# Decoder layer on one core: in the looped head groups VectorE turns the values in 32x32 blocks, and GpSimd takes their low part

## The reference, cut to what matters

```python
q = (hidden_states @ w_q).reshape(B, S, Hkv, g, D)
k = (hidden_states @ w_k).reshape(B, S, Hkv, D)
v = (hidden_states @ w_v).reshape(B, S, Hkv, D)
scores = jnp.einsum('bqhgd,bkhd->bhgqk', q, k) * scale
scores = jnp.where(causal, scores, -jnp.inf)
probs = jax.nn.softmax(scores.astype(jnp.float32), axis=-1).astype(q.dtype)
attn = jnp.einsum('bhgqk,bkhd->bqhgd', probs, v)
return attn.reshape(B, S, Hq * D) @ w_o
```

## Time and profile before

| | before |
|---|---|
| median of 3 runs | 735.61 us (734.72 to 736.96) |
| profiled execution, its own time | 735.36 us |
| its span, first to last instruction | 733.6 us |
| TensorE busy | 710.6 us, 97% |
| VectorE busy | 565.9 us, 77% |
| ScalarE busy | 379.1 us, 52% |
| GpSimd busy | 381.1 us, 52% |

### The profile page before, as it was taken

One profiled execution on the slowest core, in us unless ns is written; L12 is line 12 of the kernel. 1 busy time (PEld: TensorE's weight loads), 2 busy tenths in 40 slices (PEclk: granted clock), 3 DMA queues, 4 the chain that ended last, 5 costly groups with the idle time before them and its releaser, 6 DMA issues.

```text
span 733.6 us, 11238 instructions
## 1 busy us (share of the span) xinstructions
PE 710.6 (97%) x3494; PEld 590.4 (80%) x3494; DVE 565.9 (77%) x1166; ACT 379.1 (52%) x962; POOL 381.1 (52%) x373
## 2 busy tenths in 40 slices
PE   7999999999999999999999999999999889999994
PEld 6788888888888888888888888888887657888873
DVE  7588868876886787688768877885368878898897
ACT  4365426534643664365436535561656565655642
POOL 4565426443552555165426525542435535789885
PEclk9999999999999999999999999999999999999998
DMA  9513027204600550152035002401910002222003
GB/s 296 169 59 116 1 93 215 66 0 144 214 16 13 149 202 0 67 178 79 0 114 180 20 0 97 154 0 44 327 46 1 1 1 57 87 60 64 29 12 114
DMA packets 44901, 63.91 MB, mean 87 GB/s; under 512 B 4462, under 2 KB 23278, under 8 KB 44878
## 3 DMA queue, kind: packets, MB, share of 16 engines
q1 hardware_dynamic: 44878, 63.62, 27.4%
HBM read 52.67 MB, written 10.95 MB: 87 GB/s over the span
## 4 chain that ended last, share of the span: by engine, by line
PE 86%; DVE 6%; POOL 2%; issue 2%; ACT 2%; DMA 0%; POOLq 0%; DVEq 0%; ACTq 0%
PE psum L490 20%; PE psum L492 20%; PE psum L491 20%; PE psum L622 7%; PE psum L710 5%; PE psum L711 5%; PE psum L733 2%; PE psum L732 2%; DVE stats L1257 1%; PE psum L496 1%; PE psum L510 1%; ACT probs L912 1%; POOL o_sum L1217 1%; DVE xprobs L1383 1%; DVE negmax L1448 0%
## 5 line engine op out<-in xcount | busy, mean ns | idle before, releaser
L1154 POOL TENSOR_TENSOR probs<-probs,rowinv 128x512 f32<-128x512 f32 x64 | 76.4, 1193 | 239.7 <-DVE rowinv L1454 239.7
L1403 DVE STREAM_TRANSPOSE pt<-probs 32x128 f32<-32x128 f32 x560 | 169.0, 302 | 13.9 <-POOL pt_lo L1165 7.0
L912 ACT ACTIVATE probs<-probs,negmax 128x128 f32<-128x128 f32 x256 | 99.8, 391 | 137.9 <-DVE negmax L1448 137.9
L490 PE MATMUL psum<-xt_hi,wq_hi 128*128 128x512 f32 x256 | 103.4, 404 | 0.0
L490 PE MATMUL psum<-wo_hi,at_hi 128*128 128x512 f32 x256 | 100.4, 392 | 0.5 <-DVE at_lo L1459 0.5
L492 PE MATMUL psum<-xt_hi,wq_lo 128*128 128x512 f32 x256 | 99.9, 390 | 0.0
L491 PE MATMUL psum<-xt_lo,wq_hi 128*128 128x512 f32 x256 | 99.8, 390 | 0.0
L492 PE MATMUL psum<-wo_hi,at_lo 128*128 128x512 f32 x256 | 99.7, 390 | 0.0
L491 PE MATMUL psum<-wo_lo,at_hi 128*128 128x512 f32 x256 | 99.6, 389 | 0.0
L1393 DVE TENSOR_TENSOR xacc<-psum,xacc 128x512 f32<-128x512 f32 x64 | 44.1, 689 | 64.5 <-PE psum L492 64.5
L1165 POOL TENSOR_TENSOR pt_lo<-pt,pt_hi 128x512 fp32r<-128x512 f32 x56 | 71.9, 1285 | 27.5 <-ACT pt_hi L968 27.5
(11 more groups left out here) (149 smaller groups left out, 1530.1 us busy)
## 6 DMA issues: line engine op xcount, KB each, us to landing
wq_raw<-in_L_attn_w_q SPq DMA_DIRECT2D x8, 1024.0 KB, 5.5
wo_raw<-in_L_attn_w_o SPq DMA_DIRECT2D x8, 1024.0 KB, 7.8
u_zn<-zeros_gu SPq DMA_DIRECT2D x16, 344.0 KB, 6.4
unpacked_w<-u_q SPq DMA_DIRECT2D x8, 688.0 KB, 7.8
gw<-unpacked_w SPq DMA_DIRECT2D x20, 256.0 KB, 3.5
unpacked_w<-u_q SPq DMA_DIRECT2D x6, 512.0 KB, 6.5
u_q<-in_L_ffn_gate_qweight SPq DMA_DIRECT2D x8, 344.0 KB, 5.8
u_q<-in_L_ffn_up_qweight SPq DMA_DIRECT2D x8, 344.0 KB, 4.0
```

The source lines that it names most:

```text
L490: pe.matmul(dst, a_hi, b_hi, start=start, stop=False)
L912: e = act.activation(probs[:, t % 2, j, :], probs[:, t % 2, j, :], ACT.Exp, bias=negmax[:, t % 2, j:j + 1], accum_out=rowsum[:, t % 2, j:j ...
L1154: pool.tensor_tensor(probs[:, t % 2], probs[:, t % 2], rowinv[:, t % 2, :].unsqueeze(2).to_broadcast([P, HG, P]), ALU.mult).then_inc(prob_ ...
L1403: turned = dve.transpose(pt[keys, :, queries], probs[queries, t % 2, :, keys])
```

## The change

For the seven looped groups the turning moves from TensorE to VectorE. `vt` gets room for both halves, and a new buffer `v_raw` takes the turned block in SBUF. VectorE's new `turn_values` makes 16 transposes per half, each of 32 partitions by 4x32 elements, so that one instruction turns a 32x32 block of each of the four tiles; the table `TURN_V` deals them out over slots 2 to 5 (5, 5, 4 and 2 of them, half 1) and 8 to 10 (4, 6 and 6, half 0), at the end of VectorE's slot. ScalarE writes `v_hi` from `v_raw` at the start of its slots 6 and 11 (`SPLIT_V`), and GpSimd, no longer VectorE, subtracts: `v_lo` from `v_raw` and `v_hi`, at the start of its slots 6 and 11. For slot 11 the loops of ScalarE and GpSimd get one slot more. The first v block, ahead of the loop, and the one in `last_group` are turned by TensorE as before.

```diff
-    TURN_V = {2: 1, 6: 0}
+    TURN_V = {2: (1, 0, 5), 3: (1, 5, 10), 4: (1, 10, 14), 5: (1, 14, 16), 8: (0, 0, 4), 9: (0, 4, 10), 10: (0, 10, 16)}
+    SPLIT_V = {6: 1, 11: 0}
...
-            vt = sb("vt", [P, HALF])
+            vt = sb("vt", [P, 2, HALF])
+            v_raw = sb("v_raw", [P, BH, P])
...
@@ TensorE, group
-                    for k, i in enumerate(FILL.get(t, ())):
+                    for i in FILL.get(t, ()):
                         fill(g, i)
-                        if k == 0 and t in TURN_V:
-                            turn_values(g, TURN_V[t])
...
@@ ScalarE
+            def values_rounded(g, n):
+
+                act.wait_ge(v_turned, g * NH + (2 - n))
+                act.wait_ge(pv_done, g * NB + (0 if n == 1 else BH) + PRIME)
+                act.copy(v_hi[:, n * BH:(n + 1) * BH, :], v_raw[:]).then_inc(vt_hi, 1)
...
                 if unit == "v":
-                    act.wait_ge(vt_done, g * NH + (2 - n))
+                    act.wait_ge(vt_done, 1)
+                    act.wait_ge(v_turned, g * NH)
...
-                for t in range(SLOTS):
+                for t in range(SLOTS + 1):
+                    if t in SPLIT_V:
+                        values_rounded(g, SPLIT_V[t])
                     if t < NB:
                         exponentials(g, t)
-                    for k, i in enumerate(FILL.get(t, ())):
+                    for i in FILL.get(t, ()):
                         fill_out(g, i)
-                        if k == 0 and t in TURN_V:
-                            values_first(g, TURN_V[t])
...
@@ GpSimd, group
-                for t in range(SLOTS):
+                for t in range(SLOTS + 1):
+                    if t in SPLIT_V:
+                        half = slice(SPLIT_V[t] * BH, (SPLIT_V[t] + 1) * BH)
+                        pool.wait_ge(vt_hi, g * NH + (3 - SPLIT_V[t]))
+                        pool.tensor_tensor(v_lo[:, half, :], v_raw[:], v_hi[:, half, :].bitcast(F32),
+                                           ALU.subtract).then_inc(vt_lo, 1)
                     if t < NB:
                         normalise(g, t)
...
@@ VectorE
+            def turn_values(g, n, first, last):
+
+                if first == 0:
+                    dve.wait_ge(proj_out, g * NBLK + FIRST_BLOCKS + BLOCKS.index(("v", n)) + 1)
+                    dve.wait_ge(vt_lo, g * NH + (2 - n))
+                for k in range(first, last):
+                    i, j = divmod(k, P // QUAD)
+                    heads, keys = slice(i * QUAD, (i + 1) * QUAD), slice(j * QUAD, (j + 1) * QUAD)
+                    turned = dve.transpose(v_raw[keys, :, heads],
+                                           vt[heads, n, :].rearrange("p (a b) -> p a b", a=BH)[:, :, keys])
+                if last == (P // QUAD) ** 2:
+                    turned.then_inc(v_turned, 1)
...
                     if t < NB:
                         inverse(g, t)
-                    if t in TURN_V:
-                        values_second(g, TURN_V[t])
                     if PV <= t < NB + 1:
                         heads_second(g, t - PV)
...
                     if t in UNPACK:
                         unpack_step(g, UNPACK[t])
+                    if t in TURN_V:
+                        turn_values(g, *TURN_V[t])
```

More of the change, by code:

```diff
@@ L217, in decoder_kernel @@
         vt_done = sem("vt_done")
+        v_turned = sem("v_turned")
         vt_hi = sem("vt_hi")
@@ L506, in project, with turn_v @@
                 mm.then_inc(proj_done, 1)
-            def turn_v():
+            def turn_v(n):
                 for k in range(BH):
-                    mm = pe.transpose(psum[:, BK_VT, k * P:(k + 1) * P], vt[:, k * P:(k + 1) * P], ident[:])
+                    mm = pe.transpose(psum[:, BK_VT, k * P:(k + 1) * P], vt[:, n, k * P:(k + 1) * P], ident[:])
                 mm.then_inc(vt_done, 1)
@@ L559, in _ @@
             pe.wait_ge(ln_lo[0], NB)
-            turn_v()
+            turn_v(0)
             def out_heads(g, u):
@@ L630, in turn_values @@
                 pe.wait_ge(vt_lo, g * NH + (2 - n))
-                turn_v()
+                turn_v(n)
             def fill(g, i):
@@ L824, in project_out @@
                 cols = slice(n * HALF, (n + 1) * HALF)
-                dst = vt[:] if unit == "v" else kt[:, cols] if unit == "k" else qt[:, int(unit[1:]), cols]
+                dst = vt[:, n] if unit == "v" else kt[:, cols] if unit == "k" else qt[:, int(unit[1:]), cols]
                 if unit[0] == "q":
@@ L917, in values_first @@
             def values_first(g, n):
-                act.wait_ge(vt_done, g * NH + (3 - n))
+                act.wait_ge(vt_done, 3 - n)
                 act.wait_ge(pv_done, g * NB + (0 if n == 1 else BH) + PRIME)
                 v_first(n)
+            def values_rounded(g, n):
+                act.wait_ge(v_turned, g * NH + (2 - n))
+                act.wait_ge(pv_done, g * NB + (0 if n == 1 else BH) + PRIME)
+                act.copy(v_hi[:, n * BH:(n + 1) * BH, :], v_raw[:]).then_inc(vt_hi, 1)
             def fill_out(g, i):
```

## The result

The changed kernel takes 756.71 us (median of 4 runs, 755.17 to 758.49) against 736.29 (4 runs) beside it: ratio 1.028, 95% interval 1.027 to 1.030. It is slower, as forecast, but by 20.4 us where 10.8 were worked out, and above the whole range that was given (741 to 750.5 us).

What follows compares the result with a forecast made beforehand. TensorE's own work was taken to set the loop's pace. 735.36 - 6.65 (turning saved) + 7 x 2.49 (stalls) = 746.1; the median of runs is 0.25 above, so 746.5 us was forecast, range 741 to 750.5.

Steps and rivals of the forecast that it cites:

- TensorE loses 0.95 us per group: Slots 2 and 6: without the turning TensorE saves 0.46 and 0.49 us, 0.95 per group, 6.65 in seven.
- A turn costs 0.317 us: VectorE: each of 32 new transposes per group advances its queue by 0.317 us, 10.1 us per group.
- the rival without a stall: Turns of 0.14 us or less fit VectorE's idle time in slots 4 and 5: 729.0 us; chance 7%.
- The walk of half 1, its eight steps: Slots 2 to 6: late VectorE delays GpSimd's values' low part; TensorE waits 2.49 us before sequence 4's values.
- The net per group: Each looped group: TensorE's wait of 2.49 us less 0.95 saved, +1.54 us, seven times 10.8.
- Half 0 costs nothing: Slots 8 to 11: VectorE's turns cost nothing; GpSimd's low part is finished about 15 us before it is needed.
- GpSimd is not held up by the turns: VectorE's turns do not slow GpSimd's subtractions; the rival said 2.6 us more per group, 765 us, chance 4%.
- The clock stays up: TensorE's clock does not fall in the new gap; the rival: 15 matmuls at half speed, 770 us, chance 4%.

Runs made afterwards that it cites:

- experiment 7: The changed kernel with only half 0 turned by VectorE and subtracted by GpSimd, half 1 turned by TensorE in slot 2 as before: 733.52 us.
- experiment 3: The changed kernel with GpSimd's values' low part ahead of the weight's and slot 2's turns moved into VectorE's idle time: 729.38 us.
- experiment 1: The changed kernel with GpSimd's low part of the values (half 1) ahead of the weight's low part of slot 5: 738.42 us.
- experiment 2: The changed kernel with slot 2's five turns ahead of the low part of the first heads, in VectorE's idle time: 737.35 us.
- experiment 4: The changed kernel with nine more TensorE matmuls in slot 6, ahead of the values of sequence 4, into an unread bank: 747.10 us.

## Why the prediction was right or wrong

*TensorE loses 0.95 us per group*: right. 68.05 - 67.10 = 0.95 where nothing waits, and 0.49 for the half of experiment 7.

*A turn costs 0.317 us*: right. The five of slot 2 advance the queue by 195.34 - 193.77 = 1.57 us, and the 224 have a mean of 302 ns, where the rival without a stall needed 140 or less:

```profile
L1427 DVE STREAM_TRANSPOSE v_raw<-vt 32x128 f32<-32x128 f32 x224 | 67.7, 302 | 3.5
```

*The walk of half 1, its eight steps*: right within 0.1 us at each point that the rows above show, the place of the wait included. The net per group was 1.66 instead of 1.54, since TensorE's first matmuls after the gap stand somewhat wider apart (219.50 to the scores at 223.07 is 3.57 us, where experiment 3 has 3.40); seven times 0.12 is 0.8 us. Experiments 1, 2 and 3 move one link each, and the wait follows.

*Half 0 costs nothing*: right, shown by experiment 7.

*GpSimd is not held up by the turns*: right. Its operations take 1.27 to 1.30 us beside them.

*The clock stays up*: this is the step that failed. It was a rival with a chance of 4%, dismissed with "In the loop the gap stands between full stretches". The gap does stand so, and the clock fell all the same, in five groups of seven, for 3.4 us each and at 1.58 us apiece: 7.9 of the 9.2 to 10.2 us by which the two measurements of the kernel lie above 746.5. The walk's 0.8 us and, in the profiled execution, the 2.0 us behind the loop are the rest. The rival's price was too high in turn, seven times 3.4: it let all 15 matmuls behind the gap run slowly, and eight did. The evidence had been in the trace of before, at a place that was not read. Busy time by stretch there, behind the loop:

```profile
600.00:602.00 2.00, 1.41 (x4) 1.14 (x5) 2.00 (x4) 0.61 (x1) 0.00 (x0) 0.79 0.00 0
602.00:604.00 2.00, 2.00 (x6) 1.61 (x5) 1.90 (x4) 1.82 (x3) 0.00 (x0) 0.50 0.00 0
604.00:606.00 2.00, 2.00 (x9) 1.56 (x9) 1.93 (x3) 0.23 (x1) 0.00 (x0) 0.86 0.00 0
```

and TensorE's waits ahead of it:

```profile
596.17 0.66 PE L496 MATMUL psum<-ident,xm 128*128 128x128 f32 x4 [0.65 <-ACT xm L844]
598.53 0.66 PE L496 MATMUL psum<-ident,xm 128*128 128x128 f32 x4 [0.76 <-ACT xm L844]
600.59 0.50 PE L710 MATMUL psum<-ft_hi,gw 128*128 128x512 f32 x1 [0.94 <-DVE ft_lo L1266]
```

Here the clock went to 0.50 while TensorE was fully busy again, after a few microseconds with gaps of under 1 us each. Instead only the end of the kernel was read the earlier trace rows, where TensorE hardly works any more, and that made a falling clock look like a matter of long idleness. The same place, with the same gaps to within 0.1 us, has such a fall in four of the ten traces (before, after, experiments 2 and 4). It cost little there: the part behind the loop takes 222.9 to 223.3 us in three of the four and 222.9 to 223.0 in the six without. So these rows show that the clock can fall there, not what a fall costs in the loop. With them the rival would have deserved a fair share, at an estimated 1.7 us per fall (a stretch of 3.4 us at half the rate), and the range would have reached to about 760.

## What to carry to other kernels

Work that leaves the bound engine is gained only if its replacement is ready by the old deadline. So walk from the new producer to the consumer through every queue in between and ask where the work stands in the order: here two moves of a few instructions, into idle time and ahead of something that nobody waits for, made 729 us out of 757. A gap on TensorE can cost more than its length, because the clock may fall with it. Look for such places in the trace you have before pricing a gap at its length, and where it is as long as the gaps that did it here, price it as gap plus fall.

## What the runs showed of the hardware

The clock can fall after the gap is over: behind the gaps of 2.25 us it fell in ten groups of 14, always 0.2 to 1.4 us after TensorE had restarted, and stayed at 1.2 GHz for 3.4 us each time. With gaps of 3.5 us it fell in 7 of 7, in four of them before the restart. Gaps of 0.8, 1.0 and 1.6 us, one per group in a stretch that is otherwise full, did not bring it down in any of 21 groups, but behind the loop, where TensorE is partly idle for several microseconds, it fell in four of ten traces with no gap over 1 us (the rows of 596 to 606 us above). Which groups it hits changed between two executions of the same program with the same gaps; what decides it is open. Nine useless matmuls in the gap gained 8.6 us against the same kernel without them (755.69 and 747.10 us, on two chips, with 735.66 and 735.40 of the kernel before beside them), and three gained 7.9 (755.69 and 747.80, on one chip).
